# Sum pass of a graph kernel: two of the four row tiles of every 16th group fetched row by row from SP and ACT

## What is computed

```python
h = x @ W
msgs = h[src] * (dinv[src] * dinv[dst])[:, None]
out = segment_sum(msgs, dst) + b
x = layernorm(x + gelu(out))
```

## Time and profile before

| | us |
|---|---|
| median of 3 runs (lowest to highest) | 10384.35 (10368.25 to 10394.27) |
| the profiled execution's own time | 10294.57 |
| its span in the profile | 10292.8 |
| sum pass, first gather to last `add` | 5398.40 to 7622.4 |

### The profile page before, as it was taken

The page is one execution under the profiler, slowest core; times in us unless marked ns, Lnnn a source line. Parts: engine busy times, 40 slices in busy tenths (PEclk is TensorE's granted clock), DMA queues, the critical chain, the costliest instruction groups (busy, mean ns, idle before and its releaser), DMA issues. The chain is left out here.

```text
span 10292.8 us, 109834 instructions
## 1 busy us (share of the span) xinstructions
PE 5075.6 (49%) x27666; PEld 4241.4 (41%) x27666; DVE 5370.5 (52%) x12984; ACT 1923.5 (19%) x6462; POOL 6159.6 (60%) x6504
## 2 busy tenths in 40 slices
PE   1544444447356555555683333333345555555555
PEld 1433333335244444444562222222234554554543
DVE  4756665567466666666662222222245555555555
ACT  0000000003244444444460000000022111111114
POOL 6666666662566666655606666666645666666664
PEclk9666666667677887777795555555566767777677
DMA  4111111112344444444431111111123333333331
GB/s 108 46 46 47 46 46 46 46 46 80 97 101 99 98 99 100 99 98 97 100 83 47 46 47 46 47 46 46 47 75 108 103 101 103 102 103 102 103 102 35
DMA packets 888920, 782.03 MB, mean 76 GB/s; under 512 B 382542, under 2 KB 746790, under 8 KB 887930
## 3 DMA queue, kind: packets, MB, share of 16 engines
q0 software_dynamic: 231344, 530.57, 19.1%
q1 hardware_dynamic: 648471, 240.37, 9.6%
q10 hardware_dynamic: 8504, 4.07, 0.2%
HBM read 713.65 MB, written 60.72 MB: 75 GB/s over the span
## 5 line engine op out<-in xcount | busy, mean ns | idle before, releaser
L871 POOL DMA_INDIRECT rows_h<-t_d,idx x1563 | 1494.0, 956 | 1013.3 <-PE pn_h L1008 428.2
L520 POOL DMA_INDIRECT rows_mlp<-t_d,idx x1563 | 1477.5, 945 | 816.6 <-issue 421.2
L520 POOL DMA_INDIRECT rows_sum<-t_d,idx x1563 | 1474.4, 943 | 769.6 <-issue 447.9
L871 POOL DMA_INDIRECT rows<-t_d,idx x1491 | 1407.1, 944 | 794.9 <-issue 434.7
L1008 PE MATMUL pn_h<-S_h,rows_h 128*128 128x128 f32 x6252 | 1087.3, 334 | 335.5 <-ACT rows_h L910 166.2
L1008 PEld LDWEIGHTS pn_h<-S_h,rows_h 128*128 128x128 f32 x6252 | 1014.8, 243 | 499.3 <-issue 471.6
L910 ACT ACTIVATE rows_h<-rows_h,wc_h 128x64 f32<-128x64 f32 x4688 | 1140.7, 334 | 32.2 <-issue 20.8
L688 DVE TENSOR_TENSOR big<-big,pn_sum 128x512 f32 x391 | 269.1, 688 | 1680.2 <-remote 1472.0
L561 PE MATMUL pn_sum<-zb_sum 128*128 128x512 bf16 x391 | 210.8, 539 | 1453.7 <-DVE big L688 1387.1
L554 PE MATMUL pre_mlp<-dw_mlp,ST_mlp 128*128 128x128 f32 x3126 | 624.1, 363 | 609.4 <-DVE ST_mlp L54 438.3
L554 PEld LDWEIGHTS pre_mlp<-dw_mlp,ST_mlp 128*128 128x128 f32 x3126 | 559.0, 268 | 719.4 <-issue 712.5
(11 more groups left out here) (336 smaller groups left out, 8094.4 us busy)
## 6 DMA issues: line engine op xcount, KB each, us to landing
dw_mlp<-bd_d SPq DMA_DIRECT2D x1563, 64.0 KB
lrb_h<-lrrow_d SPq DMA_DIRECT2D x196, 128.0 KB
lrb_mlp<-lrrow_d SPq DMA_DIRECT2D x98, 256.0 KB
rows_h<-t_d,idx POOLq DMA_INDIRECT x1563
dw_h<-xp_d SPq DMA_DIRECT2D x1563, 3.0 KB
rows_sum<-t_d,idx POOLq DMA_INDIRECT x1563
rows_mlp<-t_d,idx POOLq DMA_INDIRECT x1563
rows<-t_d,idx POOLq DMA_INDIRECT x1491
```

The costliest lines, as they stand in the source:

```text
L520: e.indirect_dma_start(rows[:, g % NR, j, :], None, table, bass.IndirectOffsetOnAxis(ap=idx[:, b, t:t + 1].bitcast(I32), axis=0)).then_inc ...
L871: e.indirect_dma_start(rows[:, g % NR, j, :], None, table, bass.IndirectOffsetOnAxis(ap=idx[:, b16, t:t + 1].bitcast(I32), axis=0)).then_i ...
```

## The change

In 24 groups of the sum pass (19, 35, 51, ... 387; `FAR, EVERY = 19, 16`) POOL no longer gathers tiles 0 and 1. These 48 tiles are fetched one row at a time, 128 DMAs per tile, tile 0 from SP's queue and tile 1 from ACT's. Each DMA moves one row of 512 bytes, as two pieces of 256 bytes, from an address in a register to one partition of `frow`. The indices come as rows in SBUF (`far`): at the start of the pass SP writes 24 columns of `idx` twice to memory (`far_d`, each number by itself) and reads them back as two rows of 3072 numbers. SP and ACT load 16 of them into registers at a time. `frow` has two buffers per queue, so a queue may be one far group ahead of PE. DVE copies the landed tiles from `frow` (whose rows have a gap of two numbers) to `whole`, and PE multiplies `whole` instead of `rows`.

```diff
@@ edge_light, allocations and helpers
+            far = s("far", [64, MANY * P], I32)
+            frow = [[s(f"frow{q}{k}", [P, 2, F // 2 + 1]) for k in range(2)] for q in range(2)]
+            whole = s("whole", [P, 2, F])
+            s_row, s_far = [[sem(f"s_row{q}{k}") for k in range(2)] for q in range(2)], sem("s_far")
...
+        def apart(g):
+            return 2 if not mlp and g >= FAR and (g - FAR) % EVERY == 0 else 0
...
+        def fetch(e, engine, q):
+
+            for m in range(MANY):
+                if m >= 2:
+                    e.wait_ge(s_mm, FAR + EVERY * (m - 2) + 1)
+                for k in range(0, P, 16):
+                    r = load_values(nc, engine, far[32 * q:32 * q + 1, m * P + k:m * P + k + 16], NP - 1)
+                    for i in range(16):
+                        e.dma_start(frow[q][m % 2][k + i:k + i + 1, :, 0:F // 2],
+                                    table[bass.ds(r[i], 1), :].rearrange("o (a f) -> o a f", a=2)).then_inc(s_row[q][m % 2], 16)
@@ SP
+                for q in range(2):
+                    x = idx[:, :, :].rearrange("p b t -> p (b t)")[:, 4 * FAR + q:4 * FAR + q + 4 * EVERY * (MANY - 1) + 1:4 * EVERY]
+                    e.dma_start(d["far"][q].rearrange("m p -> p m"), x.bitcast(I32), allow_slow_non_contiguous=True).then_inc(s_far, 16)
+                e.wait_ge(s_far, 32)
+                for q in range(2):
+                    e.dma_start(far[32 * q:32 * q + 1, :], d["far"][q].rearrange("(o m) p -> o (m p)", o=1)).then_inc(s_far, 16)
...
                 e.wait_ge(s_pv, 3)
                 e.dma_start(d["deg"], deg[:, :, :]).then_inc(s_dd, 16)
                 e.wait_ge(s_dd, 16)
+                e.wait_ge(s_far, 64)
+                fetch(e, SP, 0)
@@ POOL
-                for j in range(SIZE[g]):
+                for j in range(apart(g), SIZE[g]):
@@ ACT
+        if not mlp:
+            @block.scalar
+            def _(e):
+                e.wait_ge(s_far, 64)
+                fetch(e, mybir.EngineType.Activation, 1)
@@ PE, place
-                for j in range(SIZE[g]):
+                for j in range(apart(g), SIZE[g]):
...
+                if apart(g):
+                    e.wait_ge(s_pv, 3 + (g - FAR) // EVERY + 1)
+                for q in range(apart(g)):
+                    last = e.matmul(pn[g % 2][:, bass.ds(r0[q], P)], whole[:, q, :], S[:, g % NS, q, :], start=False, stop=(q == 1))
@@ DVE, main loop
                 add(g, r0[g % 16])
+                if g + 1 < GR and apart(g + 1):
+                    m = (g + 1 - FAR) // EVERY
+                    for q in range(2):
+                        e.wait_ge(s_row[q][m % 2], 16 * P * (m // 2 + 1))
+                        last = e.tensor_copy(whole[:, q, :].rearrange("p (a f) -> p a f", a=2), frow[q][m % 2][:, :, 0:F // 2])
+                    last.then_inc(s_pv, 1)
@@ semaphores freed for the new ones
-        s_st, s_rb, s_sc, s_wn = (sem(n) for n in ("s_st", "s_rb", "s_sc", "s_wn"))
+        s_st, s_rb, s_sc = (sem(n) for n in ("s_st", "s_rb", "s_sc"))
...
-            e.wait_ge(s_wn, 32)
+            e.wait_ge(s_rb, 48)
...
-            s_zero = sem("s_zero")
...
-                if g == 0 and not gat:
-                    e.wait_ge(s_zero, 1)
```

More of the change, by code:

```diff
@@ L47 @@
 GX = 18
+FAR, EVERY = 19, 16
+MANY = len(range(FAR, GR, EVERY))
 assert B <= P and ELAST % P == 64
@@ L78, in prog @@
     deg_d = dram("deg_d", (NT, 3, P), BF16)
+    far_d = dram("far_d", (2, MANY, P), I32)
     lrn_d = dram("lrn_d", (NT, P), BF16)
@@ L106, in prog @@
         d = dict(pen=pen_d, rowpen=rowpen_d, lrrow=lrrow_d, wcol=wcol_d, x=t0_d[:, 0:F],
-                 deg=deg_d, lrn=lrn_d, t1=t1_d, t2=t2_d, t3=t3_d, xp=xp_d, own=own_d, bd=bd_d)
+                 deg=deg_d, lrn=lrn_d, far=far_d, t1=t1_d, t2=t2_d, t3=t3_d, xp=xp_d, own=own_d, bd=bd_d)
         with ExitStack() as ctx:
@@ L189, in prepare @@
         s_src, s_dst, s_w = c["s_in"]
-        s_st, s_rb, s_sc, s_wn = (sem(n) for n in ("s_st", "s_rb", "s_sc", "s_wn"))
+        s_st, s_rb, s_sc = (sem(n) for n in ("s_st", "s_rb", "s_sc"))
         PAD, CONST, SRCF, HL, CUM, REST, BASES = range(1, 8)
-        s_x, s_xo = [sem(f"s_x{i}") for i in range(4)], [sem(f"s_xo{i}") for i in range(2)]
+        s_x, s_xo = [sem(f"s_x{i}") for i in range(3)] + [s_src], [sem(f"s_xo{i}") for i in range(2)]
         block = ctx.enter_context(nc.Block())
@@ L280, in _ @@
                 e.dma_start(d[n], x[:, :]).then_inc(s_rb, 16)
-            e.wait_ge(s_rb, 64)
+            e.wait_ge(s_rb, 96)
             for row, n in ((REL, "rel"), (BASE, "base"), (QB, "qbase")):
@@ L284, in _ @@
                 e.dma_start(regs[row:row + 1, 0:x.shape[1]], x).then_inc(s_rb, 16)
-            e.wait_ge(s_rb, 112)
+            e.wait_ge(s_rb, 144)
         @block.tensor
@@ L406, in _ @@
                 score(flat[:, 16 * q:16 * q + 16, :], 16)
-    for i, n in enumerate((3, 7, 3)):
+    for i, n in enumerate((4, 7, 3)):
         c["come"][i] += 16 * n
@@ L471, in edge_light @@
         block = ctx.enter_context(nc.Block())
+        def apart(g):
+            return 2 if not mlp and g >= FAR and (g - FAR) % EVERY == 0 else 0
         def gathered(g):
-            return s_g[g % NR], landed[g % NR] + 16 * sum(SIZE[k] for k in range(g % NR, g + 1, NR))
+            return s_g[g % NR], landed[g % NR] + 16 * sum(SIZE[k] - apart(k) for k in range(g % NR, g + 1, NR))
+        def fetch(e, engine, q):
[7 more added lines that the diff above has]
+                                    table[bass.ds(r[i], 1), :].rearrange("o (a f) -> o a f", a=2)).then_inc(s_row[q][m % 2], 16)
         def windows(g):
@@ L522, in _ @@
                                          ).then_inc(s_g[g % NR], 16)
-        if mlp:
+        if not mlp:
[3 more added lines that the diff above has]
+                fetch(e, mybir.EngineType.Activation, 1)
+        else:
             @block.scalar
@@ L567, in place @@
                     e.wait_ge(sg, ng)
-                for j in range(SIZE[g]):
+                for j in range(apart(g), SIZE[g]):
                     last = e.matmul(pn[g % 2][:, bass.ds(r0[j], P)], rows[:, g % NR, j, :], S[:, g % NS, j, :],
-                                    start=False, stop=(j == SIZE[g] - 1))
+                                    start=False, stop=(j == SIZE[g] - 1 and not apart(g)))
+                if apart(g):
+                    e.wait_ge(s_pv, 3 + (g - FAR) // EVERY + 1)
+                for q in range(apart(g)):
+                    last = e.matmul(pn[g % 2][:, bass.ds(r0[q], P)], whole[:, q, :], S[:, g % NS, q, :], start=False, stop=(q == 1))
                 last.then_inc(s_mm, 1)
@@ L708, in _ @@
                 add(g, r0[g % 16])
+                if g + 1 < GR and apart(g + 1):
[4 more added lines that the diff above has]
+                    last.then_inc(s_pv, 1)
             e.drain()
     for g in range(GR):
-        c["landed"][g % NR] += 16 * SIZE[g]
+        c["landed"][g % NR] += 16 * (SIZE[g] - apart(g))
 CHAIN = ("score", "scoreT", "scan1", "row1", "scanI", "col1", "scan2", "row2", "scanJ", "col2", "scan3", "exp",
@@ L801, in edge_soft @@
             nump = ps("np", [P, 512])
-            s_ho, s_hm, s_num, s_off, s_lrn = (sem(n) for n in ("s_ho", "s_hm", "s_num", "s_off", "s_lrn"))
+            s_ho, s_hm, s_num, s_lrn = (sem(n) for n in ("s_ho", "s_hm", "s_num", "s_lrn"))
         s_gb = [sem(f"s_gb{i}") for i in range(2)]
@@ L920, in _ @@
                             n = min(512, RANKS - k)
-                            last = e.copy(acc[:, 0, k:k + n], zb[:, 0:n])
-                        last.then_inc(s_zero, 1)
+                            e.copy(acc[:, 0, k:k + n], zb[:, 0:n])
                     if step == 2:
@@ L1026, in number @@
                 e.matmul(nump[0:NT, P:P + 1], ntri[:, 0:NT], last, start=True, stop=True)
-                e.matmul(nump[0:NT, P + 1:P + 2], ones[0:NT, 0:NT], last, start=True, stop=True).then_inc(s_off, 1)
+                e.matmul(nump[0:NT, P + 1:P + 2], ones[0:NT, 0:NT], last, start=True, stop=True).then_inc(s_hm, 1)
                 e.wait_ge(s_num, 3)
@@ L1030, in number @@
                     last = e.transpose(nump[:, P + 8 + k * NT:P + 8 + (k + 1) * NT], t[:, :], ident[0:NT, 0:NT])
-                last.then_inc(s_off, 1)
+                last.then_inc(s_hm, 1)
             for i in range(-AHEAD if gat else -STEPS, GR):
@@ L1263, in number @@
                 e.drain().then_inc(s_num, 1)
-                e.wait_ge(s_off, 1)
+                e.wait_ge(s_hm, GR + 2)
                 e.tensor_copy(n["rb"][:, :], nump[0:1, 0:NT])
@@ L1280, in number @@
                 e.drain().then_inc(s_num, 1)
-                e.wait_ge(s_off, 2)
+                e.wait_ge(s_hm, GR + 3)
                 for k, x in enumerate(("degn", "grank", "gnode")):
```

6 lines of the change are left out of this document (3 added, 3 removed).

## The result

The changed kernel takes 12,296.58 us (median of four runs, 12,277.69 to 12,320.74), the kernel before 10,389.31 beside it: a ratio of 1.184 (95% interval 1.181 to 1.187), 1907 us more. The forecast was 11,190 us with a range up to 11,850: the sign was right, the size was not, and the time lies outside the range, and even above the "heavier" rival (12,080).

The account below looks back on a forecast made before the run. POOL's gathers were taken to bound the sum pass. With slower queues setting the pace, 42 + 24 x 124 + 10 = 3028 us, 804 more than 2224; added to 10384 this gives 11,190 us, range 10,560 to 11,850.

Parts of the forecast that it names:

- "heavier" rival: Sum pass: nothing gets off beside POOL, or pauses give no 0.51 us; 161 us a far group, 12,080 us; chance 5%.
- What POOL saves: POOL in the sum pass: 48 fewer gathered tiles save 60 to 68 us, 0.6 to 0.7% of the time.
- the later start: Start of the sum pass: fetching begins some 42 us after POOL's first gather; rival 1 takes some 12 us back for it.
- What costs nothing: DVE's copies (0.29 us each, 14 us in idle time), PE, DMA engine time, merged semaphores: nothing, at most 2 us.
- After POOL has stopped ... 0.51 us each: SP and ACT queues while POOL stands: 0.51 us a DMA, so the other 71 of 144 units take 36 us.
- rival 1: Sum pass: the fetch hides if a row costs under 0.6 us beside POOL, deciding at 0.61; 10,330 us; chance 12%.
- A queue gets a DMA off every 1.2 us: SP and ACT queues while POOL issues 62 tiles in 87.8 us: 1.2 us a DMA, 73 of 144 units.
- a cheap 10 us: Sum pass: a pause of POOL every 22 us, each followed by 10 us of cheap issue for the queues.
- the upper bound: Price of a row beside a busy POOL: 3.5 us, 149 us a far group, 11,790 us in all.
- The rule of the Trainium skill: DMAs from SP or ACT are immune to GpSimd descriptor interference; by it the change would be hidden and win.
- Rival 4: Sum pass: 88 + 73 = 161 us a far group, 12,080 us in all; reason given, two queues issue at once; chance 5%.
- The chain of waits: Sum pass: POOL waits for the ring, PE and DVE's copies for the rows; 24 long pauses of about 36 us.

Follow-up runs that it names:

- e1: Changed kernel with nobody fetching the 48 tiles, PE multiplying zeros and DVE copying nothing: 10,331.41 us, ratio 0.9957 to the kernel before.
- e4: Changed kernel with every POOL gather of the sum pass replaced by a memset of 128x1248, fetch kept: 10,897.83 us.
- e7: Changed kernel with the whole fetch issued but DVE, PE and POOL not waiting for it, and no copies: 12,362.57 us.
- e3: Changed kernel with each row moved as 16 pieces of 32 bytes instead of 2 of 256: 11,931.06 us, ratio 1.150 to the kernel before.
- e5: Changed kernel with row addresses fixed at build time, so no register loads or address instructions: 11,190.01 us.
- e9: Changed kernel with far tiles in every 32nd group instead of every 16th, 12 far groups and 24 tiles: 11,018.34 us.
- e10: Changed kernel with each POOL gather of the sum pass bringing 64 rows instead of 128, same number of gathers: 12,335.35 us.
- e6: Changed kernel with a POOL memset of 128x512 behind each gather of the sum pass, one gather every 1.65 us instead of 1.25: 12,094.04 us.
- e2: Changed kernel with one far tile per far group instead of two, fetched by SP, ACT fetching nothing: 12,064.03 us.
- e11: Changed kernel with 5 far groups (every 64th from 115), rows in 16 pieces, indices written after the weight loads: 10,473.0 us, ratio 1.0082 to before.

## Why the prediction was wrong in size

The step that failed is the price of a row, in both of its places in the sum: 0.51 us a unit while POOL stands measured 0.765, and 1.2 us a unit beside POOL measured 1.9. Point by point, in the order of its steps:

- **What POOL saves: right.** 60 us of gathers in the sum, 56 by e1; the later start 12, by e1 10.
- **"What costs nothing": right for the copies and the semaphores.** DVE's copy takes 0.18 us a tile (8.7 us for 48), and e1 has the merged semaphores and is faster. It was wrong in one thing that it did not list: that the rows leave POOL's gathers alone. Between far groups POOL took 98.7 us for 62 tiles (170.3 - 71.6), not 87.8, for its short waits grew from 2.8 us to 4.05 on average and took 554.6 us in place of 286.6. That is 7 of the missing 46 us (with both other prices set to their measured values).
- **"After POOL has stopped ... 0.51 us each": wrong.** Alone it would have made the forecast 11,620 us, inside the range; together with the price of the next point it is 12,130, outside. The row's price in a pause was taken from `dw_h`, a DMA with 128 pieces on 128 partitions, and was given no bounds of its own. It measured 0.86 us with the register loads (e4, e7, the pauses of the profile after), 0.765 per unit in the prediction's counting of 144. The instruction that issues the DMA alone takes 562 ns, 507 in 16 pieces (e3), and with the address fixed the whole row 0.58 (e5), so some 0.28 us of the row are its address and its loads. (The prediction's unit is a DMA or half of a register load; its 0.61 us "a row" in rival 1 is per unit, too.) With nothing else changed the period would be 87.8 + 71 x 0.765 = 142 us: 18 of the 46.
- **"A queue gets a DMA off every 1.2 us" beside POOL: wrong in size.** It was 1.98 to 2.36 us a row. Per unit: 128 rows less the 83 that fit into 71.6 us of pause at 0.86 leave 45 rows, 51 units, in 98.7 us, 1.9 us each. The last 21 of the 46 us.
- **How the hold-up works: right in kind, wrong in its times.** "An engine's instructions are held up once POOL has issued gathers for some 10 us, and are free as soon as it pauses" is what the instructions of SP show, but for the two times: the hold-up begins 4.4 us after a long pause has ended, 2 us after a short one, and it outlasts the run by 3.7 us (7058 to 7078 in the profile after). So a short pause gives the queue 3 rows in 2.0 us, not "a cheap 10 us" at 0.51, and held rows take 4.4 us, more than the 3.5 at the upper bound. Over a period the mean fits a plain sum, the queue's own 110 us plus 0.97 us for each gather issued meanwhile, with 62 or 126 of them (e9: 0.98) and with 128 or 64 rows (e10: 0.99). With other instructions, another pace or one queue it is less (e5: 0.78, e6: 0.83, e2: (160.0 - 110) / 63 = 0.79). It is a mean of this pattern of runs and pauses and no constant. Rows of before could have given about this price. SP's queue beside the run of 64 gathers of the earlier trace rows, whole batches of eight:

```profile
2684.50 29.40 SPq L847 DMA_DIRECT2D dw_h<-xp_d  x8
2714.59 0.70 SPq L841 DMA_DIRECT2D lrb_h<-lrrow_d  x1
2719.50 22.88 SPq L847 DMA_DIRECT2D dw_h<-xp_d  x8
```

  Two batches that take 4.06 us each when free took 52.3 us, 44 us too long, from POOL's last 38 gathers to 10 us behind them (2742.38, against 2732.18): some 1.2 us each. The prediction took from the same rows single prices (0.70, 3.2, 3.5) and chose between them. Its 5 DMAs in 16.10 us and 4 in 14.00 us share one DMA (2684.50 + 16.10 is later than 2699.90); the batch is 8 in 29.40, 3.7 us each.
- **The rule of the Trainium skill** ("DMA: Bandwidth & Descriptors", section "SWDGE vs HWDGE vs iDMA") that DMAs issued from SP or ACT are "immune to that interference" was rightly set below the rows. It speaks of DVE's lock on a port; here the comparison of e4 with the changed kernel shows another interference, of 0.97 us a gather, on just those queues. By the rule the period would have been the 110 us of the queue alone, 12,297 - 24 x 60 = 10,850 us, close to e4's 10,898. So the prediction's "By that rule the change would be hidden and win" does not follow: at the row's own price the change loses even then.
- **The rivals.** Rival 1 (hidden) decided at 0.61 us a unit; a unit costs 0.765 with POOL out of the way, and it had no chance. Rival 4 had the right direction on both prices and was given 5%. Its sum, 161 us, assumed that nothing gets off beside POOL and that the pause costs 0.51 a unit: the first is too hard, the second too mild, and its reason (two queues at once) was wrong by e2.
- **The chain of waits: right in every link**, with 71.6 us where 36 were forecast, 23 times on POOL (24 were forecast). The prediction had named this sign itself: pauses longer than 36 us "because 16 rows take over 8 us in them too" (they take 14). Of its two explanations for that, queues that hold each other up and landings, neither is the main one: e2 gives the first 10 us of the period, the last row lands within 1.2 us of its issue, and e3 and e5 show the price in the issue of the instruction.

With the measured prices and POOL's 98.7 us its formula gives the measured period (124 + 18 + 21 + 7 = 170), and 42 + 24 x 170.3 + 10 = 4139 us, against 4150 in the profile. The price beside POOL was worked out from this same period, so the agreement says no more than that the form of the sum holds. The form was right, its two prices were not.

What stays open: by which mechanism the gathers hold up the instructions of SP and ACT. The runs show that each instruction is held, that POOL's memsets don't do it, that half of the rows per gather changes nothing, and how much it is. They don't tell the issue on POOL from what runs in the DMA engines behind it. Open too is what in the rows lengthens POOL's waits for the ring.

## What to carry to other kernels

A price for a small DMA is not to be taken from a large one: measure an instruction of the same shape, or bound it from both sides like any unknown, the "easy" value too. Where two engines' issue disturb each other, take a mean over whole runs and pauses of the other engine rather than a price from the best and worst few, and look at single instructions for the states behind it: a mean carries over to another kernel only with the same pattern of runs and pauses. And to move work away from a bound engine that issues 1.25 us of gather for 128 rows onto queues that need 0.86 us for each row is a ratio of 88 to one: it pays only if the queue costs nothing at all, and here its mere traffic cost the bound engine eight times what it saved.

## What the runs showed of the hardware that was not expected

- Beside a run of POOL's indirect gathers each instruction on SP's and ACT's queues is held up, also one of 29 ns: one starts every 1.44 us (after) in place of every 0.28. It begins 2 to 4 us after the run does and outlasts it by 3.7 us, by 10 us behind a run of 64 gathers (before). Memsets that keep POOL busy do nothing of the kind (e4), and with 1.65 us in place of 1.25 us from gather to gather it is 0.68 us (e6).
- Over a whole period this took 0.8 to 1.0 us of the queue's time per gather (after, e2, e5, e6, e7, e9), the same for gathers of 64 and of 128 rows (e10).
- An indirect gather of 64 rows takes POOL 899 ns, one of 128 rows 946 ns (e10).
- A DMA of one 512-byte row is issued faster in 16 pieces than in two (e3: 0.775 us a row against 0.865).
- DMAs of single rows from SP and ACT lengthen POOL's waits for its ring by 0.14 us a row in 2 pieces (e7, where nobody waits for them) and 0.08 us a row in 16 pieces (e11, where no far group is waited for).
